# Low-rank FFN: an fp32r inner product over stacked parts, rows normalised three groups ahead, outputs late in the following turn

## What is computed

```python
x = x + _L1_ffn_ref(_layernorm(x, axis=-1), U1, V1, b1, U2, V2, b2)

def _L1_ffn_ref(x, U1, V1, b1, U2, V2, b2):      # U1 [256, 64], V1 [64, 1024], U2 [1024, 64], V2 [64, 256]
    P = jnp.einsum('bsd,dr->bsr', x, U1)
    H = jax.nn.gelu(jnp.einsum('bsr,rf->bsf', P, V1) + b1)
    Q = jnp.einsum('bsf,fr->bsr', H, U2)
    return jnp.einsum('bsr,rd->bsd', Q, V2) + b2
```

## Time and profile before

| what | value |
|---|---|
| median of 3 runs | 3565.01 us |
| the profiled execution's own time | 3582.19 us |
| its span on the core | 3580.1 us |
| PE busy, matmul | 2958.7 us (83%) |
| DVE busy | 2110.5 us (59%) |
| ACT busy | 1700.6 us (48%) |
| POOL busy | 1092.2 us (31%) |
| granted TensorE clock, mean | 0.909 of full |

### The profile page before, as it was taken

The page is one execution under the profiler, slowest core; times in us unless marked ns, Lnnn a source line. Parts: engine busy times, 40 slices in busy tenths (PEclk is TensorE's granted clock), DMA queues, the critical chain, the costliest instruction groups (busy, mean ns, idle before and its releaser), DMA issues. The chain is left out here.

```text
span 3580.1 us, 60274 instructions
## 1 busy us (share of the span) xinstructions
PE 2958.7 (83%) x18120; PEld 1828.1 (51%) x18120; DVE 2110.5 (59%) x4673; ACT 1700.6 (48%) x3343; POOL 1092.2 (31%) x1891
## 2 busy tenths in 40 slices
PE   6599999999983599968944999869688888797879
PEld 3234443444441588965523999734355555534433
DVE  6567677777727544444566444356476777336843
ACT  4256676776731354421112445312466667254544
POOL 3334343444401255421012445324222222120111
PEclk9679899999996799988966999989898999898889
DMA  7612222222213244330032443312211111000011
GB/s 262 221 56 76 67 77 68 79 74 77 68 62 118 76 84 91 78 72 12 0 118 59 91 92 82 69 58 82 70 52 47 49 52 45 16 0 12 0 25 35
DMA packets 170458, 248.44 MB, mean 69 GB/s; under 512 B 29208, under 2 KB 113560, under 8 KB 170288
## 3 DMA queue, kind: packets, MB, share of 16 engines
q1 hardware_dynamic: 137520, 211.67, 17.8%
q0 software_dynamic: 32768, 34.64, 6.0%
HBM read 152.81 MB, written 92.27 MB: 68 GB/s over the span
## 5 line engine op out<-in xcount | busy, mean ns | idle before, releaser
L1857 DVE CUSTOM_DVE_ANT_0 s0Ah_SD<-s0Ah_ps_s,s0Ah_table 128x1024 f32<-128x1024 f32 x512 | 607.8, 1223 | 226.7 <-PE s0Ah_ps_s L1912 181.3
L1881 ACT ACTIVATE s0Ah_PM<-s0Ah_ps_x 128x512 f32<-128x512 f32 x1024 | 536.9, 603 | 244.1 <-PE s0Ah_ps_x L1937 133.6
L1912 PE MATMUL s0Ah_ps_s<-s0Ah_plus_k,s0Ah_plus_q 48*128 48x512 f32 x1024 | 432.0, 486 | 67.9 <-DVE s0Ah_mx L1857 34.5
L1837 POOL TENSOR_TENSOR s0Ah_DG<-s0Ah_SD,s0Ah_mx 128x128 f32<-128x128 f32 x512 | 203.3, 404 | 485.8 <-DVE s0Ah_mx L1857 485.4
L1912 PEld LDWEIGHTS s0Ah_ps_s<-s0Ah_plus_k,s0Ah_plus_q 48*128 48x128 f32 x1024 | 171.2, 198 | 325.9 <-DVE s0Ah_mx L1857 219.3
L2123 ACT ACTIVATE s4Ch_PM<-s4Ch_SD,s4Ch_nb 128x260 f32<-128x260 f32 (+2 forms) x512 | 255.4, 499 | 145.4 <-POOL s4Ch_nb L2066 132.7
L1957 PE MATMUL s0Ah_ps_v<-s0Ah_PM,s0A_V 128*17 128x512 f32 x2048 | 280.1, 620 | 0.0
L2077 DVE CUSTOM_DVE_ANT_0 s4Ch_SD<-s4Ch_ps_s,s4Ch_table 128x260 f32<-128x260 f32 (+2 forms) x512 | 205.1, 408 | 83.4 <-PE s4Ch_ps_s L2168 68.1
L1937 PE MATMUL s0Ah_ps_x<-s0Ah_plus_q,s0Ah_plus_k 50*128 50x512 f32 (+3 forms) x640 | 242.0, 395 | 4.6 <-DMA s0Ah_minus_k<-s0A_parts 4.6
L2168 PE MATMUL s4Ch_ps_s<-s4Ch_ks,s4Ch_qs 96*128 96x256 bf16 (+2 forms) x896 | 144.4, 232 | 111.9 <-DVE s4Ch_mx L2077 56.1
L1937 PE MATMUL s0Ah_ps_x<-s0Ah_minus_q,s0Ah_minus_k 50*128 50x512 f32 (+3 forms) x640 | 223.0, 397 | 0.0
(11 more groups left out here) (408 smaller groups left out, 7364.0 us busy)
## 6 DMA issues: line engine op xcount, KB each, us to landing
s0A_parts<-s0Ap_sp_top SPq DMA_DIRECT2D x32, 512.0 KB, 5.4
s0A_parts<-s0Ap_sp_rest SPq DMA_DIRECT2D x32, 512.0 KB, 5.3
...
```

The costliest lines, as they stand in the source:

```text
L1837: nc.gpsimd.tensor_tensor(DG[p % 3][:, r * TB + t, :], SD[i % NSD][:, t * P:(t + 1) * P], mx[p % 3][:, r * TB + t:r * TB + t + 1].to_broad ...
L1857: nc.vector.tensor_tensor_reduce(SD[i % NSD][:, :], ps_s[i % 2][:, :, :].rearrange("p a n -> p (a n)"), table[:, (TB - 1 - t) * P:(TB - 1 ...
L1881: nc.scalar.activation(PM[n % NPB][:, :], ps_x[u % NX][:, :], ACT.Exp).then_inc(e_ok, 1)
L1912: x = nc.tensor.matmul(ps_s[i % 2][:, half, :], q[at(r), t * P:(t + 1) * P], k[at(r), half * GT:(half + 1) * GT], start=True, stop=True)
```

## The change

Only `low_rank_ffn` changes.

- U1 is loaded twice side by side (`u1` is now 128 columns wide), and `first` accumulates both halves of its contraction in one bank: `ps_p` then holds P twice, on partitions 0 to 63 and 64 to 127.
- P and V1 are split into an fp32r part and the rest. `PA` is the top part of P on all 128 partitions (ACT); `PB` has the top part on partitions 0 to 63 (ACT) and the rest on 64 to 127 (DVE, `rest_of`). `v1_top` (ACT) and `v1_rest` (DVE) are made once a stage.
- A pair of `hidden` products is now four fp32r products: `v1_top` by `PB` over 128 partitions for each m, and `v1_rest` by `PA` over 64 partitions for each m, the first m on the lower half, the second on the upper one. `ps_h` has four banks, and one semaphore step tells ACT of a pair.
- `ps_t` and `ps_o` are one bank each. The transposes of a group are made in two halves, in different places of the turn.
- `ln_h`, its moments and `ve` have two buffers. DVE and POOL normalise group g+3 in turn g (g+2 before); POOL adds b2 to group g only when group g+3 is normalised.
- The outputs of g are made in turn g+1, in two halves; DVE adds each after it.
- There are no register loops; all eight turns are written out.

```diff
@@ -159,36 +159,36 @@
 def low_rank_ffn(nc, ph, X, ident, U1, V1, b1, U2, V2, b2, out=None):
     R, FF = U1.shape[1], V1.shape[1]
     M = FF // P
+    NH = 4
     hT = ph.sb("hT", [P, 2, DC, GT])
-    u1 = ph.sb("u1", [P, DC, R])
+    u1 = ph.sb("u1", [P, DC, P])
     v1 = ph.sb("v1", [P, FF])
+    v1_top, v1_rest = ph.sb("v1_top", [P, FF], F32R), ph.sb("v1_rest", [P, FF], F32R)
...
-    PT, QT = ph.sb("PT", [P, GT]), ph.sb("QT", [P, GT])
+    PA = [ph.sb(f"PA{i}", [P, GT], F32R) for i in range(2)]
+    PB = [ph.sb(f"PB{i}", [P, GT], F32R) for i in range(2)]
...
-    ps_t = ph.ps("ps_t", [P, DC, GT])
+    ps_t = ph.ps("ps_t", [P, GT])
     ps_p = ph.ps("ps_p", [P, GT])
-    ps_h = ph.ps("ps_h", [P, 2, GT])
+    ps_h = ph.ps("ps_h", [P, NH, GT])
     ps_q = ph.ps("ps_q", [P, GT])
-    ps_o = ph.ps("ps_o", [P, 2, GT])
-    ln = LayerNorm(ph, X, ident, hT, ps_t)
+    ps_o = ph.ps("ps_o", [P, GT])
+    ln = LayerNorm(ph, X, ident, hT, None, buffers=2)
...
+    split_u1 = U1.rearrange("(c p) r -> p c r", p=P)
+    pairs = [(u1[:, :, 0:R], split_u1), (u1[:, :, R:P], split_u1), (v1[0:R, :], V1), (v1[R:P, :], V1),
...
@@ -212,111 +212,170 @@
         def _(pool):
             ln.pool_setup()
             pool.wait_ge(ln.rs, START + 1)
-            ln.pool(pool, 0)
-            ln.pool(pool, 1)
+            for g in range(3):
+                ln.pool(pool, g, g % 2)
             pool.wait_ge(weights, loaded)
-            def turn(g, h, following, more):
-                if more:
-                    ln.pool(pool, g + 2)
-                x4 = X[:, ds(g * G, G), :]
-                pool.wait_ge(ln.hrow, START + (g + 1) * G)
-                pool.sem_inc(passed, 1)
+            for g in range(NG):
+                if g < NG - 3:
+                    ln.pool(pool, g + 3, (g + 3) % 2)
+                x4 = X[:, g * G:(g + 1) * G, :]
+                pool.wait_ge(ln.hrow, START + min(g + 4, NG) * G)
                 nc.gpsimd.tensor_tensor(x4, x4, bias2[:, :].unsqueeze(1).to_broadcast([P, G, D]),
                                         ALU.add).then_inc(b_add, 1)
-            skewed_turns(pool, turn)
         @block.vector
         def _(dve):
...
+            def rest_of(g):
+                dve.wait_ge(top_ok, START + 2 * g + 2)
+                nc.vector.tensor_tensor(PB[g % 2][R:P, :], ps_p[R:P, :], PA[g % 2][R:P, :].bitcast(F32),
+                                        ALU.subtract).then_inc(rest_ok, 1)
+            def added(g, k):
+                if k == 0:
+                    dve.wait_ge(b_add, START + g + 1)
+                dve.wait_ge(o_mm, START + g * (G // 2) + k + 1)
+                x2 = X[:, g * G + 2 * k:g * G + 2 * k + 2, :]
+                nc.vector.tensor_tensor(x2, ps_o[:, :].rearrange("p (j d) -> p j d", j=2), x2,
+                                        ALU.add).then_inc(o_add, 1)
+            def rows(g):
+                ln.vector_moments(dve, g, g % 2)
+                ln.vector_rows(dve, g, g % 2)
+            rows(0)
+            dve.wait_ge(vt_ok, START + 1)
+            nc.vector.tensor_tensor(v1_rest[:, :], v1[:, :], v1_top[:, :].bitcast(F32), ALU.subtract).then_inc(vr_ok, 1)
+            rows(1)
+            rest_of(0)
+            rows(2)
+            for g in range(NG):
+                if g < NG - 3:
+                    rows(g + 3)
+                if g:
+                    added(g - 1, 0)
+                if g < NG - 1:
+                    rest_of(g + 1)
+                if g:
+                    added(g - 1, 1)
+            added(NG - 1, 0)
+            added(NG - 1, 1)
         @block.scalar
         def _(act):
+            def turned(g, c):
+                act.wait_ge(ln.trans, START + g * DC + c + 1)
+                nc.scalar.copy(hT[:, g % 2, c, :], ps_t[:, :]).then_inc(ln.hTok, 1)
+            def tops(g):
+                act.wait_ge(p_mm, START + g + 1)
+                nc.scalar.copy(PA[g % 2][:, :], ps_p[:, :]).then_inc(top_ok, 1)
+                nc.scalar.copy(PB[g % 2][0:R, :], ps_p[0:R, :]).then_inc(top_ok, 1)
+            def hidden(g, m):
+                act.wait_ge(h_mm, START + g * (M // 2) + m // 2 + 1)
+                if m == 0:
+                    act.wait_ge(q_mm, START + g)
+                nc.scalar.activation(HT[:, m, :], ps_h[:, m % NH, :], ACT.Gelu_apprx_tanh,
+                                     bias=bias1[:, m:m + 1]).then_inc(h_sb, 1)
             act.wait_ge(weights, loaded)
...
+            nc.scalar.copy(v1_top[:, :], v1[:, :]).then_inc(vt_ok, 1)
+            for g in range(2):
+                for c in range(DC):
+                    turned(g, c)
+                if g == 0:
+                    tops(0)
+            for g in range(NG):
+                for m in range(2):
+                    hidden(g, m)
+                if g < NG - 2:
+                    turned(g + 2, 0)
+                for m in range(2, 6):
+                    hidden(g, m)
+                if g < NG - 1:
+                    tops(g + 1)
+                for m in range(6, 8):
+                    hidden(g, m)
+                if g < NG - 2:
+                    turned(g + 2, 1)
                 act.wait_ge(q_mm, START + g + 1)
                 act.wait_ge(o_mm, START + g * (G // 2))
                 nc.scalar.copy(QT[:, :], ps_q[:, :]).then_inc(q_sb, 1)
...
         @block.tensor
         def _(pe):
-            pe.wait_ge(weights, loaded)
-            def first(g, h):
+            def turned(g, c):
+                if c == 0:
+                    pe.wait_ge(ln.hrow, START + (g + 1) * G)
+                pe.wait_ge(ln.hTok, START + g * DC + c)
+                for j in range(G):
+                    x = nc.tensor.transpose(ps_t[:, j * P:(j + 1) * P], ln.h[g % 2][:, j, c * P:(c + 1) * P], ident[:, :])
+                x.then_inc(ln.trans, 1)
+            def first(g):
                 pe.wait_ge(ln.hTok, START + (g + 1) * DC)
...
+                pe.wait_ge(top_ok, START + 2 * g)
+                pe.wait_ge(rest_ok, START + g)
+                for c in range(DC):
+                    x = nc.tensor.matmul(ps_p[:, :], u1[:, c, :], hT[:, g % 2, c, :], start=(c == 0), stop=(c == DC - 1))
+                x.then_inc(p_mm, 1)
             def hidden(g, m):
-                pe.wait_ge(h_sb, START + g * M + m - 1)
-                nc.tensor.matmul(ps_h[:, m % 2, :], v1[:, m * P:(m + 1) * P], PT[:, :],
-                                 start=True, stop=True).then_inc(h_mm, 1)
+                if m == 0:
+                    pe.wait_ge(rest_ok, START + g + 1)
+                pe.wait_ge(h_sb, START + g * M + m + 2 - NH)
+                for j in range(2):
+                    nc.tensor.matmul(ps_h[:, (m + j) % NH, :], v1_top[:, (m + j) * P:(m + j + 1) * P], PB[g % 2][:, :],
+                                     start=True, stop=False)
+                for j in range(2):
+                    half = slice(j * R, (j + 1) * R)
+                    x = nc.tensor.matmul(ps_h[:, (m + j) % NH, :], v1_rest[half, (m + j) * P:(m + j + 1) * P],
+                                         PA[g % 2][half, :], start=False, stop=True)
+                x.then_inc(h_mm, 1)
             def down(g, m):
+                if m == 0:
+                    pe.wait_ge(q_sb, START + g)
                 pe.wait_ge(h_sb, START + g * M + m + 2)
                 for j in range(2):
-                    i = nc.tensor.matmul(ps_q[j * R:(j + 1) * R, :], u2[:, m + j, :], HT[:, m + j, :],
+                    x = nc.tensor.matmul(ps_q[j * R:(j + 1) * R, :], u2[:, m + j, :], HT[:, m + j, :],
                                          start=(m == 0), stop=(m == M - 2), tile_position=(0, j * R))
                 if m == M - 2:
...
+                    x.then_inc(q_mm, 1)
+            def outs(g, k):
+                n = g * (G // 2) + k
                 pe.wait_ge(q_sb, START + g + 1)
...
+                pe.wait_ge(o_add, START + n)
+                for j in range(2):
+                    at = (2 * k + j) * P
+                    x = nc.tensor.matmul(ps_o[:, j * D:(j + 1) * D], QT[:, at:at + P], v2[:, :], start=True, stop=True)
+                x.then_inc(o_mm, 1)
+            pe.wait_ge(weights, loaded)
+            turned(0, 0)
+            turned(0, 1)
+            first(0)
+            turned(1, 0)
+            turned(1, 1)
+            pe.wait_ge(vr_ok, START + 1)
+            for g in range(NG):
+                hidden(g, 0)
+                if g < NG - 2:
+                    turned(g + 2, 0)
+                hidden(g, 2)
+                down(g, 0)
+                hidden(g, 4)
+                if g:
+                    outs(g - 1, 0)
+                down(g, 2)
+                if g < NG - 1:
+                    first(g + 1)
+                hidden(g, 6)
+                if g:
+                    outs(g - 1, 1)
+                if g < NG - 2:
+                    turned(g + 2, 1)
+                down(g, 4)
+                down(g, 6)
+            outs(NG - 1, 0)
+            outs(NG - 1, 1)
```

(47 more changed lines are left out.)

24 lines of the change are left out of this document (4 added, 20 removed).

## The result

The changed kernel takes 3547.5 us (median of 20 runs; one of them, a disturbed one at 3974 us, is left out of the ratio) against 3567.39 us (median of 20). The ratio is 0.9943, interval 0.9925 to 0.9962: 0.6% faster, within the 1% that this measurement tells from no change. The forecast was 3542 us, a ratio of 0.9936 to the median then at hand.

What follows compares the result with a forecast made beforehand. PE, busy 117.74 of 118 us in stage s5, was taken as the bound. Stage gains of 10.6 and 12.1, together 22.7 us, took the profiled 3582.19 to 3559.5, scaled to a median of 3542; 8-in-10 range 3519 to 3564.

Steps and rivals of the forecast that it cites:

- to the transposes of group 2: Stage start: from PE's first transposes until the rows of group 2 are ready for PE, 14.05 us.
- rest of turn 0, with the clock: Turn 0 after the transposes of group 2, without outputs: 9.9 us, plus 2 for the clock at half.
- the end: Stage end: 4.7 us against 3.37 now, with 0.2 ahead and 1.1 for outputs waiting on the first add.
- later start: Before PE's first transposes: the weight wait ends later by one more load, at most 1.4, estimated 0.6 us.
- The turn: Steady turn on PE, summed block by block: 12.91 us, 2.44 less than 15.35.
- I take 0: Steady turn, `down` 0: PE's wait for the second gelu is 0 to 0.1 us, counted as 0.
- One of the signs given: PE's turn: the L325 rows, the fp32r `v1_top` products of `hidden`, would stand 0.23 us apart.
- The start: Stage start: PE newly waits about 3 us for group 2's rows; half clock costs 0 to 4, taken as 2.
- Cheap changes to row halves: `hidden` in the steady turn: five shape changes at no cost, 1.0 us a turn, giving 3526 us; chance 0.22.
- Halves one after the other: `hidden`: the 64-partition products run in sequence, four times 0.23 us a turn, giving 3557 us; chance 0.06.
- PE waiting 0.5 for ACT twice a turn: Second gelu 0.5 us late ahead of `down` 0 and `down` 6; turn 13.9, giving 3558 us; chance 0.07.
- The slow clock: Several turns at half clock, some 10 us more each; four in each stage give 3618 us; chance 0.07.

Runs made afterwards that it cites:

- e2: Changed kernel with the second part of the `hidden` product over all 128 partitions, zeros in half its weights, instead of row halves; 3556.16 us in one run.
- e8: Changed kernel with only PE's order within a turn changed: first outputs half behind `hidden` 2, `down` 0 and 2 together behind `hidden` 4; 3521.28 us in one run.
- e1: Changed kernel with DVE's rows of group 1 ahead of `v1_rest`, group 2 ahead of `rest_of(0)`; 3534.95 us in one run, later median of 7 3537.48, ratio 0.988.
- e3: Changed kernel's order and buffers with the old arithmetic: fp32 PT, `first` on column halves, `v1` unsplit; 3558.29 us in one run.
- e6: Changed kernel with the edits of e1, e2 and e8 together; 3518.53 us, median of 6 runs, ratio 0.9859 to the kernel before.
- e5: Changed kernel with DVE and POOL normalising group g+2 in turn g instead of g+3, POOL's bias add one group earlier; 3562.23 us in one run.

## Why the prediction was right, step by step

The stage's sum against stage s5 after, counted from PE's first transposes:

| term | predicted | measured |
|---|---|---|
| to the transposes of group 2 | 14.05 | 13.91 |
| rest of turn 0, with the clock | 9.9 + 2 | 11.74 |
| turns 1 to 5 | 64.55 | 64.82 |
| turn 6, turn 7 | 12.5, 10.8 | 12.52, 10.81 |
| the end | 4.7 | 5.29 |
| stage | 118.5 | 119.09 |
| later start | 0.6 | 0.63 |

- *The turn*, 12.91 against 12.96. The prices drawn from the earlier trace rows hold block by block. e2, which takes seven changes away and pays only 0.04 for each of its four pairs over 128 partitions (0.47 for 0.43), came at 12.67, and e8, with two changes less, at 12.59. Two blocks were off and nearly cancel: transposes 0.41 for 0.50, the pair behind them 1.12 for 0.99. Most of that is only where the border between them lies: in e8, where `down` 0 stands elsewhere, they take 0.41 + 1.08 = 1.49, and 0.50 + 0.99 is 1.49 too. The 0.04 left over is the step "I take 0": `down` 0 does wait for the second gelu, at the low end of the 0 to 0.1 given. e2 brought this wait to light, by taking away what covered it. One of the signs given did not come in its words: the L325 rows are not 0.23 apart but 0.34. The sum had the 0.10 for this, the sign had not.
- *The start.* The wait was foreseen at about 3 and measured at 3.35; the cause (rows of group 2 behind `rest_of(0)`) and its clock cost (2 foreseen, 1.85 by e1) are both shown. That the cost came so near is partly luck: the 2 was the middle of a range of 0 to 4 that no row narrowed, and in the ten stages with the wait the half clock lasted anything from 3.4 to 10.2 us. So is the later start, 0.63 for 0.6: in the other stages with nine loads the same stretch took 10.03 to 11.02 us, 0.3 to 1.2 more than in the same stage before, and with eight loads (e3) 10.02 and 9.40.
- *The end* is the term that was furthest off, 0.6 too small; the five steady turns add 0.27. The steps of the end were right: where the clock stays (e1, s7 of e6) the tail from the QT copy is 4.54 to 4.55, which with the 0.11 ahead of it is 4.65. The clock's second fall, which came in six of the 18 stages, is what I had left out. What decides whether it comes stays open.
- *The whole.* 21.5 us by the stages, 22.7 forecast, 19.9 between the medians (the interval of the ratio spans 13.6 to 26.8).

The rivals. Cheap changes to row halves, with only column tiles paying: excluded by the turn of 12.96, where this rival has 11.9, and by e2, since taking the row halves away would then have made the turn longer. e8 does not bear on it, as the changes that it takes away are to and from column halves. Halves one after the other: excluded by the L329 rows, two products over 0.43. PE waiting 0.5 for ACT twice a turn: it waits 0.04 ahead of `down` 0 and not at all ahead of `down` 6, where the four `down` take 1.87 without a gap. The slow clock: steady turns ran at 1.00 throughout, but e5 shows that the mechanism is real: its waits of 1.94 a turn brought the clock down in some turns, which cost 1.5 each, not the 10 of my rival, in which a whole turn ran at half.

The Trainium skill, TensorEngine Tiling (Array Packing), section Tiling Modes, says that a change of mode drains TensorE. e8 agrees in that a change costs time, and prices it: two changes of shape fewer, about 0.33 us. The Trainium skill, TensorE: Matmul & The Clock Gate, section on HAM oscillation, has waits between bursts bring the half clock back. The start of the stage agrees, and e5 does at three of its five waits of 1.94 to 2.08 us in s5; the steady turns of the changed kernel, without such waits, do not fall under it.
